# Moving one exponential down the ScalarE queue: behind the shared units, in front of both Softplus

## Time and profile before

| | |
|---|---|
| median of 3 runs | 887.07 us (886.49 to 888.79) |
| the profiled execution, its own time | 887.37 us |
| its span, first to last instruction | 885.4 us |
| PE busy | 770.7 us, 87% of the span |
| PEld busy | 660.7 us, 75% |
| DVE busy | 654.1 us, 74% |
| ACT busy | 569.0 us, 64% |
| POOL busy | 300.8 us, 34% |
| mean granted TensorE clock | 0.961 of full speed |

### The profile page before, as it was taken

How to read it: one execution, slowest core, us unless ns; L and a number is a source line. 1 busy time by engine, 2 the same in 40 slices (tenths; PEclk the granted TensorE clock), 3 DMA queues, 4 the chain that set the end, 5 groups by cost and what they waited for, 6 DMA issues and landing times.

```text
span 885.4 us, 14581 instructions
## 1 busy us (share of the span) xinstructions
PE 770.7 (87%) x4784; PEld 660.7 (75%) x4784; DVE 654.1 (74%) x1516; ACT 569.0 (64%) x1354; POOL 300.8 (34%) x393
## 2 busy tenths in 40 slices
PE   4768898998989989989988989989999899899885
PEld 3547687777878778878877877877878787787774
DVE  3644678788788787787787787887787887877752
ACT  4545558658568567667676676586585675666553
POOL 1222233333333343252243343333333333432321
PEclk9757999999999999999999999999999999999997
DMA  9000000000000000000000000000000000000000
GB/s 344 19 0 1 1 1 13 1 13 13 1 13 13 1 13 13 2 12 1 13 12 1 13 13 1 13 13 1 13 12 2 7 7 1 7 3 6 6 7 13
DMA packets 8154, 14.12 MB, mean 16 GB/s; under 512 B 849, under 2 KB 7049, under 8 KB 7569
## 3 DMA queue, kind: packets, MB, share of 16 engines
q1 hardware_dynamic: 8080, 13.20, 4.3%
HBM read 10.05 MB, written 3.15 MB: 15 GB/s over the span
## 4 chain that ended last, share of the span: by engine, by line
DVE 39%; PE 30%; ACT 15%; issue 10%; POOL 5%; DMA 0%; DVEq 0%; POOLq 0%; SPq 0%; ACTq 0%
PE pa L427 6%; DVE work L1079 6%; PE ctl L450 5%; DVE hm_hi L1025 5%; PE ctl L466 4%; DVE work L1055 3%; PE pb L427 3%; DVE gl L1039 3%; ACT ge L806 3%; DVE xf L1170 2%; ACT mexp L836 2%; DVE hm_hi L1032 2%; DVE work L1060 2%; PE cd L427 2%; DVE work L1062 2%
## 5 line engine op out<-in xcount | busy, mean ns | idle before, releaser
L347 POOL TENSOR_TENSOR hm_lo<-gl,mexp 128x256 fp32r<-128x256 f32 x144 | 115.3, 822 | 356.6 <-DVE gl L1039 356.6
L450 PE MATMUL ctl<-w2e_hi,hm_hi 128*128 128x512 f32 (+1 forms) x432 | 163.6, 388 | 14.9 <-DVE hm_hi L1025 14.7
L450 PE MATMUL ctl<-w2e_lo,hm_hi 128*128 128x512 f32 (+1 forms) x432 | 150.7, 361 | 0.0
L1025 DVE TENSOR_TENSOR hm_hi<-ge,mexp 128x256 fp32r<-128x256 f32 x144 | 80.7, 585 | 65.8 <-ACT mexp L836 55.4
L824 ACT ACTIVATE work<-ctl 128x256 f32<-128x256 f32 (+1 forms) x144 | 70.1, 487 | 69.8 <-PE ctl L469 69.4
L450 PEld LDWEIGHTS ctl<-w2e_hi,hm_hi 128*128 128x128 f32 x432 | 82.3, 190 | 35.5 <-DVE hm_hi L1025 23.2
L466 PE MATMUL ctl<-w2e_hi,hm_lo 128*128 128x512 f32 (+1 forms) x432 | 102.7, 364 | 0.0
L427 PE MATMUL pa<-x1T,par 128*128 128x128 f32 x768 | 92.6, 280 | 0.0
L427 PEld LDWEIGHTS pa<-x1T,par 128*128 128x128 f32 x768 | 91.1, 198 | 0.0
L450 PEld LDWEIGHTS ctl<-w2e_lo,hm_hi 128*128 128x128 f32 x432 | 82.5, 191 | 10.8
L466 PEld LDWEIGHTS ctl<-w2e_hi,hm_lo 128*128 128x128 f32 x432 | 73.8, 188 | 15.7 <-POOL hm_lo L347 1.7
(11 more groups left out here) (168 smaller groups left out, 1739.1 us busy)
## 6 DMA issues: line engine op xcount, KB each, us to landing
work<-params_dram SPq DMA_DIRECT2D x3, 1152.0 KB, 9.8
out_dram<-y SPq DMA_DIRECT2D x24, 128.0 KB, 1.7
xa<-x_dram SPq DMA_DIRECT2D x16, 128.0 KB, 2.2
par<-params_dram SPq DMA_DIRECT2D x1, 1280.0 KB, 12.4
work<-params_dram SPq DMA_DIRECT2D x2, 512.0 KB, 10.9
xa<-x_dram SPq DMA_DIRECT2D x8, 119.0 KB
par<-params_dram SPq DMA_DIRECT2D x1, 512.0 KB, 15.5
par<-params_dram SPq DMA_DIRECT2D x1, 465.0 KB, 3.9
```

The lines of the kernel that those rows point to most:

```text
L347: TT(hm[1][:, j, c, :], gl[:, c, :], pairs(tile, j, c), ALU.mult).then_inc(done, 1)
L450: mm(dst[:, a:z], hm[0][:, j, c, :], w2e[i][:, c, a:z], start=(c == 0 and i == 0), stop=False)
L1025: V.tensor_tensor(hm[0][:, j, c, :], ge[:, c, :], pairs(tile, j, c), ALU.mult).then_inc(done, 1)
```

## The change

Step 3 of the list above moves behind step 7. The load of the Gelu set between Exp and what follows is left out where a tile t exists, since the load of the Softplus set comes right behind. Before, a full slot goes Gelu, Exp, Gelu, Softplus, Gelu: four loads. After, it goes Gelu, Exp, Softplus, Gelu: three loads. No arithmetic changes, and no other engine's queue is touched.

```diff
                 if t.exists():
                     unit(t, 1, u1_sb, u1_ps, ctl[1], 2)
+                if t.exists():
+                    unit(t, 2, u1_sb, u1_ps, ctl[0], 2)
+
+                if n.exists():
+                    state(x1T, 2 * D, n, x1T_ps, x1T_sb, e2_ps)
+
+                if z.exists():
+                    passed(act, xT_ps, z)
+                    AF(xT[:, :, :].rearrange("p k m -> p (k m)"), pc[:, 0:D], ACT.Copy).then_inc(xT_sb, 1)
+
+                if n.exists():
+                    shared_units(n, s2_ps, s2_sb, sh2, sab2, halt2_ps, sl2_v)
+
                 if e.exists():
                     if t.exists():
                         nc.scalar.preload_act_table_set("exp_and_others")
                     passed(act, smax_v, e)
                     passed(act, eT_ps, e, back=1)
                     AF(ex[:, :], sc[:, :], ACT.Exp, scale=-1.0, bias=nmx[:, e.s:e.s + 1],
                        accum_out=esum[:, e.s:e.s + 1]).then_inc(ex_sb, 1)
-                    if f.exists():
+                    if f.exists() and not t.exists():
                         nc.scalar.preload_act_table_set("gelu_and_others")
-                if t.exists():
-                    unit(t, 2, u1_sb, u1_ps, ctl[0], 2)
-
-                if n.exists():
-                    state(x1T, 2 * D, n, x1T_ps, x1T_sb, e2_ps)
-
-                if z.exists():
-                    passed(act, xT_ps, z)
-                    AF(xT[:, :, :].rearrange("p k m -> p (k m)"), pc[:, 0:D], ACT.Copy).then_inc(xT_sb, 1)
-
-                if n.exists():
-                    shared_units(n, s2_ps, s2_sb, sh2, sab2, halt2_ps, sl2_v)
 
                 if t.exists():
                     softplus_of(m, t)
```

More of the change, by code:

```diff
@@ L865, in slot @@
                     unit(t, 1, u1_sb, u1_ps, ctl[1], 2)
-                if e.exists():
-                    if t.exists():
[L868 to L872, removed]
-                    if f.exists():
-                        nc.scalar.preload_act_table_set("gelu_and_others")
                 if t.exists():
@@ L886, in slot @@
                     shared_units(n, s2_ps, s2_sb, sh2, sab2, halt2_ps, sl2_v)
+                if e.exists():
+                    if t.exists():
+                        nc.scalar.preload_act_table_set("exp_and_others")
+                    passed(act, smax_v, e)
+                    passed(act, eT_ps, e, back=1)
+                    AF(ex[:, :], sc[:, :], ACT.Exp, scale=-1.0, bias=nmx[:, e.s:e.s + 1],
+                       accum_out=esum[:, e.s:e.s + 1]).then_inc(ex_sb, 1)
+                    if f.exists() and not t.exists():
+                        nc.scalar.preload_act_table_set("gelu_and_others")
                 if t.exists():
```

## The result

The changed kernel takes 905.75 us (median of 4 runs, 905.29 to 906.52), the kernel before 887.77 us beside it (4 runs). The ratio is 1.0204, with a 95% interval of 1.0187 to 1.0222: 2% slower. The forecast was 906.0. The profiled execution has a span of 904.7 us (885.4 before) and a granted TensorE clock of 0.951 (0.961 before).

What follows compares the result with a forecast made beforehand. A loop of VectorE's half and TensorE's half bounds the kernel, with ScalarE's side branch all but critical at its end. 887.4 + 23.6 - 4.7 = 906.3, less 0.3 for the median: 906.0 us, own range 900 to 912.

Steps and rivals of the forecast that it cites:

- The loop: Full slot: VectorE from its first mask to xf, then TensorE to the next masks; ScalarE's block is a side branch.
- The front: Start of ScalarE's branch: x1T starts 0.48 us earlier, passed on to TensorE but not to VectorE.
- The back: Behind ScalarE's shared units: Softplus load, ge and gh come 1.33 us later; gl moves by that less its room.
- The sum: Whole kernel: 20 slots with a tile n grow by 23.6 us together, slots 0 and 1 give -4.7.
- The wait of sc: VectorE's sc of z waits for the later Exp, 0.2 us in slot 12, beside the later ge; priced at nothing.
- The clock: New TensorE idle before L450 and L673 drops its clock in every slot: +12, 918 us; chance 0.11.
- idle time before L673 some 0.5 longer: Sign that the forecast is right: TensorE waits some 0.5 us longer before the transposes of xf.
- The number of loads: ScalarE's queue sets the pace, so 22 fewer loads of 1.283 us give 859 us; chance 0.05.
- TensorE sets the period: Only the later xf's excess over TensorE's 0.64 us idle before L673 counts: +5, 892 us; chance 0.08.
- It is hidden: A wait not seen takes up some of ge's delay, gains and losses cancel: 885 to 890 us; chance 0.04.

Runs made afterwards that it cites:

- e3: Kernel before with Exp's place kept, both its loads gone where a tile t exists (Tanh in place of Exp, results wrong): 874.0 us, ratio 0.9847.
- e9: Changed kernel with six matmuls of 128x256, result unused, in TensorE's wait for hm_hi: 903.9 us, ratio 1.0173.
- e10: Kernel before with four matmuls of 128x256, result unused, in front of the transposes of x1 (L576): 885.5 us, ratio 0.9968.
- e7: Kernel before, nothing moved, with one more Exp-set load directly in front of the Softplus load in 22 slots: 912.9 us, ratio 1.0278.
- e2: Changed kernel with two buffers for sc, used in turn, so VectorE's sc need not wait for Exp: 902.3 us, ratio 1.0158.
- e6: Kernel before with Exp and its load moved in front of n's unit 1, Gelu load behind xfT, two sc buffers: 873.5 us, ratio 0.9829.
- e4: Changed kernel without the Exp-set load where a tile t exists (Tanh in place of Exp, results wrong): 874.5 us, ratio 0.9839.
- e1: Changed kernel with the Gelu load put back behind Exp, four loads a slot: 953.3 us, ratio 1.0703.
- e8: e1 with ten matmuls of 128x256, result unused, in TensorE's wait for hm_hi: 934.3 us, ratio 1.0517.

## Why the prediction was right

- *The loop.* That a full slot's chain goes over VectorE and not over ScalarE's block is shown by e3: in 19 full slots 49 us of loads less on ScalarE, 3.3 us less time, and those are the clock's.
- *The front.* 0.48 was to be passed on to TensorE and end there. The wait of L589 fell by 0.48, and no full slot got shorter by it.
- *The back.* 1.33 later less a room of 0 to 0.22. From e9 less e10 it is 1.16 a slot; e7 gives the same with a load alone.
- *The sum.* Slots 2 to 21 were forecast at +23.6 and came at +22.3, slots 0 and 1 at -4.7 and -4.7. The second agreement is partly luck. In slot 1 the wait in front of L589 did fall by the 2.6 of the forecast (3.51 to 0.89). But the slot also lost the half-clock stretch that it had from 75.4 to 82.2 (the 32 matmuls into pa took 4.97 and take 3.73), and ge, which had waited 1.94 for them, now starts right behind its load (81.10). The 1.2 us gained by this was given back ahead of L576, which started 20.72 behind the slot's start and starts 21.99 behind it. None of this was in the forecast. Ahead of slot 0 I took 0 for a possible gain; it was +1.1, because L652 ran at half clock there (2.05 in place of 1.10). The order is not the cause: e10, with the order of before, has L652 at 2.04 and begins slot 0 at 23.5, and e2, with the new order, at 21.4. Behind slot 21 came another +0.6. That the total is met to 0.3 us is luck too: these 1.7 us more than made up for the 1.3 that slots 2 to 21 had too many.
- *The wait of sc* was priced at nothing in a full slot; e2 shows it, for the 3.7 us that it came to in 19 of them.
- *The clock* (rival 3) did act, at less than half of its price. The gap in front of L450 became 1.82 (forecast 1.9) and half-clock stretches moved from the place around x1T to the place behind the wait for hm_hi, in 10 of 19 full slots and not in all. I had 0.6 for each; it is 2.4 / 10 = 0.24. I had set the idle time before L673 against it at 1.1; without a stretch it is 0.94 to 1.05, and with one it is used up. So the sign "idle time before L673 some 0.5 longer" came true in no slot: it is 0.3 longer in nine and gone in ten. In the kernel before a stretch cost 0.8, as it lay in the branch itself. The two sums, 3.2 gone and 2.4 come, nearly cancel, which the forecast had taken for granted.
- *The number of loads* (rival 1) is refuted by the result itself, and by e6: 22 loads more than the changed kernel, 32 us less. The rule of the Trainium skill to batch activations by set (page "ScalarE: Activation LUTs", section "Table sets: the hidden batching unit") holds for ScalarE's busy time, which fell by 26 us, and says nothing of the place. The drain that the Trainium skill adds to each switch (same page, section "What ACT_TABLE_LOAD costs") is not seen: Exp starts at 462.74, 0.02 behind the end of its load.
- *TensorE sets the period* (rival 2) is refuted by the growth of 1.16 a slot, where it had 1.11 - 0.64 = 0.47, and by e9 and e10: more work on TensorE, less time. *It is hidden* (rival 4) falls with the same growth.

What I sized wrongly were the experiments that free the first slots: e3, e4 and e6 gained 9 to 11 us there where I had counted 5. In the trace of e6, slots 0 to 2 are 3.8, 5.6 and 1.1 shorter, and slot 1 has no half clock where before had one from 75 to 82 us. A part of that is ScalarE's work itself, which e6 takes out of slot 1's branch and the change put back behind it. How the 11 divide between the two was not tried.

## What to carry to other kernels

A move that takes work out of a queue's busy stretch is worth what its successors stood waiting for it, and costs what it adds in front of the next consumer: read both gaps, in front of the first instruction that gets earlier and behind the last that gets later, before counting what is saved. Here the first was 0.48 of 3 us and led nowhere, the second had 0.2 us of room and took 1.33. Work with a switch of tables belongs where its engine waits for others, even if that takes one more switch; e6 found two such waits and was 32 us faster than the changed kernel with one load more in each slot; the 15 us against the kernel before came almost all from the first slots and the clock. Where an engine off the loop idles longer, look at what follows: TensorE came back at half clock.

## What the runs showed of the hardware

A wait of TensorE can cost more than its length. In e1, with 3.11 us of idle time in front of L450, the granted clock was 0.50 for 6.8 us in each of the 19 full slots of the profiled execution, from inside that wait on. Ten useless matmuls (4.5 us) in its place took these stretches away: 22 us less in the full slots and 19 us less in the whole kernel. With 1.8 us of idle (the changed kernel) it was half clock for 3.4 us in 10 of 19 slots, and in the other nine, with the same idle time, it was not. In the kernel before, with 1.08 and 0.78 us of idle close to each other, it was so in 4 of 19. A table load took 1283 ns in every group, and one on the loop cost 1.28 us a slot (e8 less e9).
